# Two-layer transformer kernel on one core: attention scores from stacked parts, a three-slot score ring, and a scan product with its operands exchanged

## The reference

```python
def step(h, inp):
    x_t, dt_t, B_t, C_t = inp
    dA = jnp.exp(dt_t * A)
    h = h * dA[:, :, None, None] + (dt_t[:, :, None] * x_t)[..., None] * B_t[:, None, None, :]
    y = jnp.einsum('bhpn,bn->bhp', h, C_t)
    return (h, y)
```

```python
attn_weights = jnp.einsum('bhtd,bhsd->bhts', q * scaling, k) + mask      # 8 maps, causal
attn_weights = jax.nn.softmax(attn_weights.astype(jnp.float32), axis=-1)
aw = attn_weights.reshape(B, H, 2, T, T)
diff = aw[:, :, 0] - lambda_full * aw[:, :, 1]
attn = jnp.einsum('bhts,bhsd->bhtd', diff, v)
normed = a32 * jax.lax.rsqrt(jnp.mean(a32 * a32, axis=-1, keepdims=True) + 1e-05)
```

## Time and profile before

| | us |
|---|---|
| median of 3 runs | 1725.51 |
| lowest, highest | 1722.6, 1728.06 |
| profiled execution | 1726.24 |
| its span | 1724.2 |
| scan, window 220 to 360 | 140 |
| Laplace stage, window 1118 to 1195 | 77 |
| attention, window 1195 to 1452 | 257 |

### The profile page before, as it was taken

The page is one execution under the profiler, slowest core; times in us unless marked ns, Lnnn a source line. Parts: engine busy times, 40 slices in busy tenths (PEclk is TensorE's granted clock), DMA queues, the critical chain, the costliest instruction groups (busy, mean ns, idle before and its releaser), DMA issues. The chain is left out here.

```text
span 1724.2 us, 24943 instructions
## 1 busy us (share of the span) xinstructions
PE 1430.5 (83%) x8810; PEld 1167.2 (68%) x8811; DVE 998.2 (58%) x1843; ACT 591.6 (34%) x1166; POOL 439.4 (25%) x350
## 2 busy tenths in 40 slices
PE   8663889985996868989989999868999997837993
PEld 3233466674893348988989999725777776537993
DVE  2666868757545665555455445583777775234553
ACT  3212633322222133422323334224555554214550
POOL 0001078724000036065043040440000000033763
PEclk9886889987997568999999999989999998968997
DMA  5000000001000013012002000000000000244333
GB/s 208 0 0 1 13 1 1 1 1 49 1 1 0 1 49 133 14 49 98 0 4 93 0 0 0 12 13 1 1 1 1 1 1 1 74 158 170 134 115 106
DMA packets 25083, 64.90 MB, mean 38 GB/s; under 512 B 4194, under 2 KB 16372, under 8 KB 20082
## 3 DMA queue, kind: packets, MB, share of 16 engines
q1 hardware_dynamic: 23474, 59.84, 9.7%
q0 software_dynamic: 1536, 4.10, 0.7%
HBM read 54.07 MB, written 9.44 MB: 37 GB/s over the span
## 5 line engine op out<-in xcount | busy, mean ns | idle before, releaser
L1418 ACT ACTIVATE hT<-ps,eb 128x256 f32<-128x256 f32 x296 | 124.2, 471 | 289.3 <-PE ps L1273 289.3
L1436 DVE CAST ehidh<-hT 128x512 fp32r<-128x512 f32 x148 | 79.6, 538 | 100.9 <-ACT hT L1418 100.9
L1674 ACT ACTIVATE pr<-ps,nmax 128x256 f32<-128x256 f32 (+7 forms) x128 | 94.1, 738 | 110.9 <-DVE nmax L1704 110.6
L1438 DVE TENSOR_TENSOR ehidl<-hT,ehidh 128x512 fp32r<-128x512 f32 x148 | 124.9, 844 | 5.1
L1617 PE MATMUL ps<-kT,qT 128*128 128x512 f32 (+3 forms) x320 | 119.0, 478 | 1.5 <-ACT pr L1674 1.5
L1444 DVE SCALAR_TENSOR_TENSOR X<-ps,wE,X 128x256 f32 x74 | 35.9, 485 | 113.6 <-PE ps L1273 104.0
L1704 DVE TENSOR_REDUCE nmax<-ps 128x1 f32<-128x256 f32 (+7 forms) x128 | 93.4, 752 | 10.8 <-PE ps L1621 9.9
L1273 PE MATMUL ps<-hTh,ew_0h 128*128 x288 | 83.9, 291 | 18.5 <-issue 18.5
L1273 PE MATMUL ps<-hTh,ew_1h 128*128 x304 | 85.8, 282 | 9.5 <-issue 9.5
L1273 PE MATMUL ps<-ew_1h,ehidh 128*128 128x256 f32 x304 | 86.0, 283 | 4.3 <-DVE ehidl L1438 4.0
L1273 PE MATMUL ps<-hTh,ew_1l 128*128 x304 | 85.1, 280 | 0.0
(11 more groups left out here) (490 smaller groups left out, 4205.6 us busy)
## 6 DMA issues: line engine op xcount, KB each, us to landing
ew1s<-in_ew_dram SPq DMA_DIRECT2D x9, 1024.0 KB, 4.7
ew2s<-in_ew_dram SPq DMA_DIRECT2D x9, 1024.0 KB, 6.5
fw1s<-in_fw_dram SPq DMA_DIRECT2D x8, 1024.0 KB, 5.1
fw2s<-in_fw_dram SPq DMA_DIRECT2D x8, 1024.0 KB, 7.5
slot_rows<-zero SPq DMA_DIRECT2D x1, 2560.0 KB, 8.8
xr<-slot_rows SPq DMA_DIRECT2D x5, 512.0 KB, 6.3
xT<-in_xT_dram SPq DMA_DIRECT2D x4, 512.0 KB, 7.7
X<-in_x_dram SPq DMA_DIRECT2D x1, 2048.0 KB, 16.5
```

What stands on the lines that cost most here:

```text
L1418: nc.scalar.activation(hid[:, f, :], ps[:, f // 2, (f % 2) * JOB:(f % 2 + 1) * JOB], ACT.Gelu, bias=b1[q][:, f:f + 1]).then_inc(k.e_act, 1)
L1436: nc.vector.tensor_copy(hi[:, f, :], hid[:, f, :]).then_inc(k.e_dhi, 1)
L1438: nc.vector.tensor_tensor(lo[:, f, :], hid[:, f, :], hi[:, f, :], ALU.subtract).then_inc(k.e_lo, 1)
L1674: nc.scalar.activation(pr[:, n % 3, u, 0:wide], half(n, u, wide), ACT.Exp, bias=nmax[:, n % 2, u:u + 1], accum_out=sums[:, u, n:n + 1]).th ...
```

## The change

In the lists below a line number is that of the program the list is from.

**The scan.** `k.dtA` is split into two parts, `dth` (rounded to the fp32r type) and `dtl` (the rest). The stationary operand is now the triangle `gt` in fp32r, and the masked matrices are the moving one: POOL makes the first part (128x1024, as before), ACT the second by 8 activations of 128x128. PE has 4 products of 512 columns where it had 8 float32 products of 128, each of two instructions. The gated result goes to `k.post` in place of two other tiles. DVE has three small instructions more in the phase before.

**The Laplace stage.** Keys and queries are split into a high and a low part. SP then copies 32-row pieces by DMA so that one map's operands lie on 96 rows: high, low, high of the keys (`kst`), high, high, low of the queries (`qst`). For each of 4 token windows that is 24 DMAs of 64 KB for the keys, in all 96, and 24 DMAs of 16 KB for each tile's queries, of which 48 for the first two tiles stand between window 1 and window 2 of the keys. The block now ends after all `kst` DMAs have landed. POOL's clearing of qT is gone, and the load of `wo` is moved behind the attention.

**The attention.** One fp32r product on 96 rows replaces the float32 score product. The mask is written first, the scores are added. Scores lie in three slots of two banks each (one bank for each map, up to 512 columns), so that a unit with more than 4 key blocks takes two slots. DVE takes the maxima of both maps in one instruction; where a unit's slots cannot be read as one piece it takes two and combines them, and ACT's exponentials are then four. For odd units POOL computes the difference by two instructions. PE's transposes and value products run 3 units behind, through one transpose bank and one result bank. POOL squares the results. The queries' stack holds two tiles; the DMAs of tile i wait until the scores of tile i-2 are done. DVE's list has the maxima of a unit before the difference of the unit before it for c below 4, and behind it from c = 4 on.

SP's list at the Laplace stage, before. The names are the four weight loads; behind them comes the end of the block.

The core of the diff:

```diff
-                for q in range(NH):
-                    last = nc.tensor.matmul(ps[:, SEG + q // 4, (q % 4) * P:(q % 4 + 1) * P], G[:, i % 2, q, :],
-                                            k.const("le"), start=(q % 4 == 0), stop=True, skip_group_check=True)
+                for q in range(2):
+                    for n, part in enumerate(Gp):
+                        last = nc.tensor.matmul(ps[:, SEG + q, :], k.gtr[:, :],
+                                                part[:, i % 2, 4 * q:4 * q + 4, :].rearrange("p h t -> p (h t)"),
+                                                start=(n == 0), stop=(n == 1))
...
+            def masked_remainders(i):
+                if i >= 2:
+                    act.wait_ge(k.m_seg, i - 1)
+                for q in range(NH):
+                    last = nc.scalar.activation(Gp[1][:, i % 2, q, :], k.const("le"), ACT.Copy,
+                                                scale=k.dtl[:, i * NH + q:i * NH + q + 1])
+                last.then_inc(k.m_Gl, 1)
...
+            for w in range(NW):
+                tok = slice(w * W, (w + 1) * W)
+                sp.wait_ge(k.l_kl, EB * (w + 1))
+                for s in range(8):
+                    r, f = slice(32 * (s % 4), 32 * (s % 4) + 32), s // 4
+                    for at, src in ((0, kh), (32, kl), (64, kh)):
+                        sp.dma_start(k.kst[at:at + 32, s, tok].bitcast(F32),
+                                     src[r, w % 2, f, :].bitcast(F32)).then_inc(k.s_kst[w], 16)
+                if w == 1:
+                    sp.wait_ge(k.l_ql, EB)
+                    for i in range(2):
+                        load_query_stack(sp, k, i)
+            for w in range(NW):
+                sp.wait_ge(k.s_kst[w], 16 * 24)
 
...
+                    if w >= 2 and f == 0:
+                        act.wait_ge(k.s_kst[w - 2], 16 * 24)
+                    nc.scalar.copy(kh[:, w % 2, f, :], ps[:, bank(w, f), :]).then_inc(k.l_k, 1)
...
+def load_query_stack(sp, k, i):
+
+    tok = slice(i * P, (i + 1) * P)
+    for s in range(8):
+        r, f = slice(32 * (s % 4), 32 * (s % 4) + 32), s // 4
+        for at, src in ((0, k.qh), (32, k.qh), (64, k.ql)):
+            sp.dma_start(k.qst[at:at + 32, i % 2, s, :].bitcast(F32), src[r, f, tok].bitcast(F32)
+                         ).then_inc(k.s_qst[i % 2], 16)
...
+        for n in range(UNITS):
+            c = unit(n)[1]
+            mine = []
+            for at in range(0, (c + 1) * P, chunk(n)):
+                mine.append((len(slots) % RING, at, min(chunk(n), (c + 1) * P - at)))
+                slots.append(n)
+            joined = len(mine) == 2 and mine[0][0] < RING - 1 and mine[0][2] == mine[1][2]
+            pieces = [(mine[0][0], 0, (c + 1) * P)] if joined else mine
+            segments.append([(len(owner) + g, *piece) for g, piece in enumerate(pieces)])
+            owner += [n] * len(pieces)
+            evicted.append([segments[slots[len(slots) - len(mine) + g - RING]][-1][0] + 1
+                            if len(slots) - len(mine) + g >= RING else 0 for g in range(len(mine))])
...
+        @block.sync
+        def _(sp):
+            for i in range(2, NT):
+                sp.wait_ge(k.a_qk, segments[HEADS * (i - 2) + HEADS - 1][-1][0] + 1)
+                load_query_stack(sp, k, i)
...
+                if h == 0:
+                    pe.wait_ge(k.s_qst[i % 2], 16 * 24 * (i // 2 + 1))
+                for g, at in enumerate(range(0, wide, chunk(n))):
+                    r = (segments[n][0][1] + g) % RING
+                    w = min(chunk(n), wide - at)
+                    if evicted[n][g]:
+                        pe.wait_ge(k.a_exp, 2 * evicted[n][g])
+                    own = at + w == wide
+                    if own:
+                        for u in range(2):
+                            nc.tensor.matmul(ps[:, 2 * r + u, w - P:w], identb[:, :], maskb[:, :], start=True,
+                                             stop=False, skip_group_check=True)
+                    for u in range(2):
+                        s = 2 * h + u
+                        last = nc.tensor.matmul(ps[:, 2 * r + u, 0:w], k.qst[0:96, i % 2, s, :],
+                                                k.kst[0:96, s, keys + at:keys + at + w], start=not own, stop=True,
+                                                skip_group_check=True)
+                    if own or len(segments[n]) == 2:
+                        last.then_inc(k.a_qk, 1)
+
+            def turn(n, g):
...
+                act.wait_ge(k.a_max, n + 1)
+                if n >= KEEP:
+                    act.wait_ge(k.a_tr, first[n - KEEP + 1])
+                for s, r, at, w in segments[n]:
+                    for u in range(2):
+                        out = rows[n % KEEP][:, u, at:at + w]
+                        if w > W:
+                            out = out.rearrange("p (g t) -> p g t", g=2)
+                        nc.scalar.activation(out, halves(n, r, w)[:, u], ACT.Exp,
+                                             bias=nmax[:, n % KEEP, u:u + 1],
+                                             accum_out=sums[:, u, s:s + 1]).then_inc(k.a_exp, 1)
+
...
+            def largest(n):
+                if n >= KEEP:
+                    dve.wait_ge(k.a_exp, 2 * (segments[n - KEEP][-1][0] + 1))
+                mine = segments[n]
+                for g, (s, r, at, w) in enumerate(mine):
+                    dve.wait_ge(k.a_qk, s + 1)
+                    out = nmax[:, n % KEEP, :] if len(mine) == 1 else part[:, g, :]
+                    last = nc.vector.tensor_reduce(out, halves(n, r, w), AX.XY if w > W else AX.X, ALU.max,
+                                                   negate=True)
+                if len(mine) == 2:
+                    then(last)
+                    last = nc.vector.tensor_tensor(nmax[:, n % KEEP, :], part[:, 0, :], part[:, 1, :], ALU.min)
+                last.then_inc(k.a_max, 1)
 
...
+                then(nc.vector.reciprocal(rec[:, :, n], total))
+                then(nc.vector.scalar_tensor_tensor(rr[:, n % KEEP:n % KEEP + 1], total[:, 0:1], rec[:, 1, n:n + 1],
+                                                    lam[:, 67:68], ALU.mult, ALU.mult))
+                if n % 2:
+                    dve.sem_inc(k.a_rr, 1)
+                    return
+                nc.vector.scalar_tensor_tensor(rows[n % KEEP][:, 0, 0:wide], rows[n % KEEP][:, 1, 0:wide],
+                                               rr[:, n % KEEP:n % KEEP + 1], rows[n % KEEP][:, 0, 0:wide], ALU.mult,
+                                               ALU.add).then_inc(k.a_d, 1)
...
+            for n in range(UNITS + LAG + 1):
+                if n > LAG and (n - LAG) % HEADS == 0:
+                    collect((n - LAG) // HEADS - 1)
+                if n < UNITS and unit(n)[1] < 4:
+                    largest(n)
+                if 0 < n <= UNITS:
                     difference(n - 1)
-                largest(n, 0)
-                largest(n, 1)
-                if n % HEADS == 2 and n > 2:
...
+            def difference(n):
+                wide = (unit(n)[1] + 1) * P
+                both = rows[n % KEEP]
+                pool.wait_ge(k.a_rr, n // 2 + 1)
+                nc.gpsimd.tensor_scalar(both[:, 1, 0:wide], both[:, 1, 0:wide], rr[:, n % KEEP:n % KEEP + 1], None,
+                                        ALU.mult).then_inc(k.a_sc, 1)
+                pool.wait_ge(k.a_sc, n // 2 + 1)
+                nc.gpsimd.tensor_tensor(both[:, 0, 0:wide], both[:, 0, 0:wide], both[:, 1, 0:wide],
+                                        ALU.add).then_inc(k.a_dp, 1)
```

More of the change, by code:

```diff
@@ L1606, in scores @@
                 i, c, h = unit(n)
                 keys = (i - c) * P
-                before = n - 1 if c >= 4 or (n and unit(n - 1)[1] >= 4) else n - 2
-                if before >= 0:
-                    pe.wait_ge(k.a_exp, 2 * before + u + 1)
-                s = 2 * h + u
-                q = k.qT[:, s, i * P:(i + 1) * P]
-                out = half(n, u, (c + 1) * P)
-                for at in range(0, c * P, W):
-                    to = min(at + W, c * P)
-                    nc.tensor.matmul(out[:, at:to], q, k.kT[:, s // 4, keys + at:keys + to], start=True, stop=True)
@@ L1645, in _ @@
             pe.wait_ge(k.a_mask, 2)
[L1646 to L1648 removed]
+            for n in range(UNITS + LAG):
+                if n >= LAG:
+                    turn(n - LAG, 0)
                 if n < UNITS:
[L1650 to L1653 removed]
+                    scores(n)
+                if n >= LAG:
+                    if len(groups(n - LAG)) == 2:
+                        turn(n - LAG, 1)
+                    product(n - LAG)
         @block.scalar
```

298 lines of the change are left out of this document (171 added, 127 removed).

## The result

| | before | changed kernel |
|---|---|---|
| median (runs) | 1726.22 us (4) | 1818.07 us (4) |
| lowest, highest | 1722.6, 1728.06 | 1815.41, 1819.49 |
| ratio | | 1.0533, 95% interval 1.0511 to 1.0555 |
| span of the profiled execution | 1724.2 | 1815.6 |
| granted clock, mean | 0.901 | 0.813 |

A forecast was written before the change was run, and what follows sets the result against it. PE was taken to set the pace before, with SP's DMA lists and a serial attention loop limiting next. Scan -15, Laplace +17, small tiles -5, large tiles +29, end +3 gave +29: 1755 us, range 1718 to 1788.

The forecast's parts named there:

- small tiles: Attention tiles of 1 to 4 key blocks: SP's DMA lists replace PE as limit, 42 and 45 us, together -5 us.
- The scan: Scan: PE's list gets 0.97 us shorter per block, to a period of 7.6 us; gain 15 us.
- large tiles: Attention tiles of 5 to 8 key blocks: post-exponential work, maxima and exponentials run in series; +14.3 us a batch, +29 for both.
- Two small DMAs follow each other by 0.47 us, whatever they carry: SP's lists in Laplace stage and small tiles: fixed issue spacing, so 24 DMAs take 11.3 us.
- The two kinds of stage end: Laplace stage: key copies charged by bytes, 1.05 us each, +40; or with 1.9 us fixed landing, 0.58 each, +18.
- the +17: Laplace stage: the increase taken for its end, near the estimate with fixed landing time.
- The range's upper bound of 40: Laplace stage: the most its end was allowed to move later, in us, with copies charged whole by bytes.
- waits of the combination for POOL: Large tiles: DVE's combination of two maxima waits 0.75 to 0.9 us for POOL's difference; 3.9 us a batch.
- PE was to be busy below 70%: Attention from 5 blocks on: a sign that the forecast is right, with ACT waiting for maxima.
- The price of POOL's halves: Large tiles, odd units' difference: POOL's sum alone 2.18 us for 1024, with the scaling some 3.4.
- The end: Attention's end: POOL's slower difference, one more unit in flight and the square on POOL; +3 us.
- The third rival: Key pieces land by bytes, +23 us, and PE gets its lower clock in much of the attention; 1778 and more, 14%.

The follow-up runs named there:

- e3_forms: The changed kernel with other forms (fewer rows or columns, DRAM source) in the same lists of 24 DMAs; 1843.5 us, one run, only SP's spacing read.
- e4_dense: The changed kernel with each transpose of the attention made twice; 1811.7 us, ratio 1.0487.
- e6_half_maxima: The changed kernel with maxima over only the first half of each piece's columns in tiles of 5 to 8 blocks; 1785.8 us, ratio 1.0343.
- e7_split: e2_few_dmas with large tiles taken apart: no slots joined, each slot freed after its own exponentials, maxima before the previous unit's difference; 1721.0 us, ratio 0.9968.
- e5_odd_on_dve: The changed kernel with POOL's two instructions for odd heads' differences made one DVE instruction; 1822.7 us, ratio 1.0551.
- e8_split_dense: e7_split with each transpose made twice; 1711.6 us, ratio 0.9922.
- e9_two_queues: e8_split_dense with keys' parts copied directly again, high pieces by SP, low pieces and the queries' stores by POOL; 1708.5 us, ratio 0.9858.
- e2_few_dmas: The changed kernel with key and query parts written to DRAM whole and read back stacked, in far fewer DMAs; 1754.8 us, ratio 1.015.
- e11_one_input: e8_split_dense with DVE's two small combinations written as reductions over one tile; 1701.5 us, ratio 0.9857.

## Why the prediction was wrong, step by step

- **Direction and stages: right, but for the small tiles.** The scan is a gain, Laplace and large tiles a loss, and SP is late next in the Laplace stage and the small tiles. These were to gain 5 us and lost 27.
- **The step that failed** is "Two small DMAs follow each other by 0.47 us, whatever they carry". They follow by 0.634 when both ends are in SBUF (e3_forms). In the Laplace stage that is 144 x 0.164 = 24 us: start 1124.3, as forecast once the scan's gain is taken off, and end 1218.5. The two kinds of stage end that I weighed, by bytes or by fixed landing, were both beside the point: a 64 KB piece landed after 2.0 us, and the 4 us of the +17 that were for them did not come. The range's upper bound of 40 for the stage happened to cover it; nothing covered the same error in the tiles behind.
- **Small tiles: SP as forecast, the same term too small, and one wait left out.** 24 issues are 15.2 us in place of 11.3. In the working, tile 4 then starts at 4.5 + 3 x 15.2 + 2 = 52.1 in place of 40.4, 53.7 as the rows count (54.8 measured), and the second batch's 45 become 60.6 (64.5 measured). Behind the other 4 us is a wait that the working left out: it had SP issue the lists of tiles 9 to 12 in one go from tile 7's last scores, but the list of tile 10 waits for tile 8's, and SP stands 7.8 us. Tile 8's scores stand in PE's list behind tile 7's value products, at the low clock; e4_dense, where these are short, has 1.7 us there. So tiles 10, 11 and 12 waited, where 9, 10 and 11 were to. The landing is paid once, as forecast.
- **Large tiles: right in size, partly by cancellation.** +15.9 us for the first batch against +14.3. A loop through DVE and the slots is there (e6_half_maxima, e7_split), though e5_odd_on_dve shows that a difference on DVE is not wholly in it. But 3.9 us of the 14.3 (its own terms give 4.0 to 4.8) were waits of the combination for POOL, of which 1.4 us in all occurred. A sign failed here too: PE was to be busy below 70%, and it was busy 86 of 95 us at the low clock. The price of POOL's halves was wrong: the scaling takes 1.9 to 2.8 us and does not hold DVE, the sum comes only behind it, and by then the combination was over, as here in the changed kernel (DVE, then POOL):

```profile
1354.27 0.16 DVE L1835 TENSOR_TENSOR nmax<-part 128x2 f32<-128x2 f32 x1
```

```profile
1351.82 2.84 POOL L1888 TENSOR_SCALAR pr<-pr,rr 128x1024 f32<-128x1024 f32 x1 [7.01 <-DVEq L1850]
```

  Some 5 us of a batch came instead from other terms; e4_dense gives 2 of them to the clock. The Trainium skill, "SBUF — State Buffer", section "Who interferes with whom", read as "any GpSimd instruction that reads SBUF", does not agree with six combinations that ran through POOL's scaling at 0.16 us; for its two-input sum, it agrees to 0.02 us, and size is no excuse, as the prediction said.
- **The end: too small.** From the last ratio to the end of the last value product it is 16.6 us where before it was 5.4, +11 and not +3. There the clock is not free: e8_split_dense and e9_two_queues have the same attention, and from tile 15's first ratio to its end it took 27.3 us where the clock stayed at 1.00 and 36.1 where it was 0.57 over the last 27. In the table this counts +6 for the attention's end, since the second batch is taken as the first.
- **The third rival** had the low clock right (0.54), and put no figure on it. e4_dense gives it 7 us in tiles 4 to 15 of the profile, 6 by the medians, and the end comes on top: up to 9, by the split kernels. Its other half, landing by bytes, did not happen. It is the rival that was nearest, at 1778 and more, and its 14% were too few.
- **The scan: right.** The period is 7.70 us, not 7.6, which makes the gain 13.6 and not 15; the 13.2 measured agree, as far as 3 us of scatter tell.
- With 0.634 in place of 0.47 and nothing else changed, the working's +29 grows by 6 x 3.9 = 23 in the Laplace stage and by 27 in the small tiles: +79, 1805. The other 13 us are SP's pause and slower steps in the small tiles (5), the end at a low clock and what is behind it (5.5), 3 in the large tiles and 2 in the scan, less the 3 that did not come in the Laplace stage.

## What to carry to other kernels

Price an instruction from a row of its own form: for a DMA that means where source and destination lie, and a single such row (0.53 beside 0.43) outweighs two tidy ones of another kind. When a term is multiplied by 144 in one stage and by 24 in each small tile behind, its error is the forecast's error, so give it bounds before any finer argument. And when two engines alternate through too few buffers, look first at what stands between them in the list (which maximum before which difference, which slot freed by what) before making either faster: that was worth some 31 to 34 us here.

## What the runs showed of the hardware that was not expected

- SP issues a copy from SBUF to SBUF every 0.61 to 0.67 us (two rows or 32, 64 columns or 512), one from DRAM to SBUF every 0.47 (e3_forms), and a store of a part from SBUF to DRAM was followed after 0.43 (e2_few_dmas).
- With POOL issuing too (0.49 to 0.56 each) and the DMA engines 0.79 busy, SP's spacing was 0.754 (e9_two_queues).
- POOL's scaling of 128x1024 by a column (one tile read) takes 2.84 us, its sum of two tiles 2.35 (changed kernel).
- A DVE instruction of two elements a row with two SBUF inputs waits for the end of POOL's two-input sum when it starts inside it (0.27 to 1.53 us long in e8_split_dense); six that ran beside the one-input scaling did not wait (0.16, changed kernel); and 32 written as a reduction of one tile did not either (e11_one_input).
- Work added to PE in its gaps shortened the kernel: 9 us in e8_split_dense and, less surely, 6 in e4_dense, with the granted clock up from 0.80 to 0.96 and from 0.54 to 0.79 in the large tiles.
